# Neighbour maximum: the end of a search with other VectorE operations, a table of x with swapped blocks, and one maximum along the later ring slots

## The chip, the cores and the metric

The kernel runs on one core of one Trainium2 chip. The metric is the device time of one execution in microseconds (us); lower is better.

## What is computed

Four graph layers run over the same adjacency matrix of 8192 x 8192 (about 0.4% ones, the diagonal included) and rows x of 8192 x 128. The change lies wholly in the first layer, which takes for every row the maximum of x over the row's neighbours, adds it to x and normalises:

```python
def _L0_gnn_ref(X, adj):
    mask = adj != 0
    def body(_, mrows):
        vals = jnp.max(jnp.where(mrows[:, :, None], X[None, :, :], neg), axis=1)
        has_nbr = jnp.any(mrows, axis=1)
        return (None, jnp.where(has_nbr[:, None], vals, jnp.zeros((), X.dtype)))
...
x = _layernorm(x + _L0_gnn_ref(x, adj), axis=-1)
x = _layernorm(x + _L1_gnn_ref(x, L1_gnn_W, L1_gnn_a, adj, 8192), axis=-1)
x = _layernorm(x + _L2_gnn_ref(adj, x, L2_gnn_W, L2_gnn_a), axis=-1)
x = _layernorm(x + _L3_gnn_ref(x, adj, L3_gnn_W, L3_gnn_a), axis=-1)
```

## The kernel before

The first layer is `neighbour_max`. It walks the 64 tiles of 128 rows of the adjacency matrix, one phase for each tile. SyncE loads a tile (4 MB) in four pieces. TensorE turns it (`turn`, L470) in eight steps of eight 128x128 blocks, ScalarE makes the signs (L426) and stores them as the mask of the later layers.

The neighbours of a row are treated in two ways. Each row's columns are cut into 512 words of 16. The first neighbour in a word goes through matmuls: `firsts_of` (L489) marks it, ScalarE makes it clean (`lone`, L413), and `sum_pair` (L503) multiplies it by x in three bf16 parts into the PSUM tile `sums`. VectorE takes the maximum of `sums` and the running `top` (`pair`, L601). There are eight such pairs in a phase, called here pairs 0 to 7 (`step(0)` to `step(7)` in the code). The tile `sums` is there once, so `sum_pair` of the next pair waits on `sums_used` until VectorE has read it, and `pair` waits on `sums_ready`.

The further neighbours in a word are found by a search on VectorE, between the pairs of the phase after the tile's turning. From the counts per word it makes keys (L680 to L711), takes the eight largest words with several (L713), peels off three powers of two from each (loop over `d`, L729 to L740), and sorts the keys with MAX8 and MATCH_REPLACE8 to 24 slots (`srt`, L748 to L755). Then it works out the row numbers in `idx` (L759 to L768), which groups of slots are needed (`need`, L764), and the number found (L766). `Steps` (`steps`, `side`, `tree`) are semaphores by which one VectorE operation waits for an earlier one: `settle()` waits for all that was issued on that chain.

GpSimd gathers those rows (L352, one indirect DMA for a slot) out of `x_ext`, a copy of x in DRAM with 128 extra rows of the lowest value for empty slots, into `ring`, 24 slots of 128 values for each partition. A group of slots that no row needs is filled by a memset (L388). Two phases after the search VectorE takes the maximum over the slots: slots 0 to 11 in halves (L606, then `into`, L613), and slots 12 to 23 in the same manner in the second half of the phase, between pairs 3 and 5. `rest_ready` says that slots 12 to 23 are filled, `rest_free` that they may be filled anew.

The order on each engine is the order of the code; TensorE's is written in its `phase`, VectorE's in the `phase` below. TensorE's matmul L477, which adds up `need`, stands ahead of L489 and L503 of pair 0 of the next phase, and waits for `need_made`. In the last four phases (`quad == NC - 1`) no tile is turned any more.

The other three layers start at about 1710 us of the span and the diff doesn't touch them.

Of the kernel before, what the change touches and what calls it, by code (L numbers as in the profile page):

```python
# [8 lines left out]
I32 = mybir.dt.int32  # L9
# [3 lines left out]
ALU = mybir.AluOpType  # L13
ACT = mybir.ActivationFunctionType
AXX = mybir.AxisListType.X

P = 128
N = 8192
F = 128
T = N // P  # L20
# [3 lines left out]
NW = N // WORD  # L24
EXPONENT = 0x7F800000
TOP_BIT = 2.0 ** WORD
MORE = 8
# [50 lines left out]
def hold(eng, sem, value):  # L78


    eng.wait_ge(sem, value)
    if not isinstance(value, int):
        eng.sem_inc(SPARE[0], 1)
# [96 lines left out]
def neighbour_max(nc, x, adj, mask_t, x_ext, nm, deg, consts, constants):  # L180
# [14 lines left out]
    with ExitStack() as ctx:  # L195
# [17 lines left out]
        bit = stats[:, 0:SRT, 1].bitcast(I32)  # L213
        base = sb("base", [P, SRT], I32)
        pad = sb("pad", [P, SRT], F32)
# [112 lines left out]
        def _(pool):  # L328
# [3 lines left out]
            pool.dma_start(x_ext[P:P + N, :], x).then_inc(x_copied, 16)  # L332
            pool.wait_ge(low_ready, 1)
            pool.dma_start(x_ext[0:P, :], top[:, 0, 0:F]).then_inc(low_in, 16)
# [7 lines left out]
            pool.wait_ge(x_copied, 16)  # L342
# [224 lines left out]
        def _(dve):  # L567
# [9 lines left out]
            nc.vector.memset(top_bit[:, :], TOP_BIT).then_inc(opens_free, 1)  # L577
            steps.do(nc.vector.memset(need[:, :, :], 0.0))
# [54 lines left out]
            def between(n):  # L633

                if n == LOWEST_AT:
                    dve.wait_ge(top_used, NC - 1)
                    dve.wait_ge(lower_free, T - TC + 1)
                    dve.wait_ge(rest_free, T - TC + 1)
                if LOWEST_AT <= n < LOWEST_AT + NC - 1:
                    lowest_of(n - LOWEST_AT)  # L640
# [12 lines left out]
            def phase(t, k, extracts=True, finishes=True, quad=None, tops=True):  # L653
# [6 lines left out]
                def bits(ap):  # L660
                    return ap.bitcast(I32)
# [56 lines left out]
                if finishes:  # L718
                    hold(dve, rest_ready, old + 2)
                    tree.did(larger(h, h, h + h // 2, h // 2))  # L720
# [3 lines left out]
                if finishes:  # L724
                    tree.did(larger(h, h, h + h // 4, h // 4))
                for d in range(DEEP - 1):
                    if extracts:
                        steps.settle()
                        steps.did(nc.vector.tensor_scalar(bits(many_high[:, d, :]), bits(y), EXPONENT, None, ALU.bitwise_and))  # L729
                    if d == 0:  # L730
                        step(4)
                    if finishes and d == 1:
                        tree.did(larger(h, h, h + 1, 1))
                    if finishes and d == 2:
                        tree.did(larger(h, h, h + 2, 1))
                    if extracts:
                        steps.settle()
                        if d + 1 < DEEP - 1:
                            steps.did(nc.vector.tensor_tensor(out=y, in0=y, in1=many_high[:, d, :], op=ALU.subtract))
                        side.did(nc.vector.tensor_tensor(out=bits(keys[:, NW + d * MORE:NW + (d + 1) * MORE]), in0=bits(many_high[:, d, :]), in1=many_no[:, :], op=ALU.bitwise_or))  # L740
                if finishes:
                    tree.settle()
                    hold(dve, lower_free, old + 2)
                    into(old, None, h).then_inc(rest_free, 1)
                if extracts:
                    side.settle()
                    steps.settle()
                    steps.did(nc.vector.max(out=srt[:, 0:8], in_=keys[:, :]))  # L748
# [8 lines left out]
                if extracts:  # L757
                    steps.settle()
                    steps.did(nc.vector.tensor_scalar(bit, bits(srt[:, :]), 23, None, ALU.logical_shift_right))  # L759
                    steps.did(nc.vector.tensor_scalar(base[:, :], bits(srt[:, :]), NW - 1, 4, ALU.bitwise_and, ALU.logical_shift_left))  # L760
                    side.did(nc.vector.tensor_scalar(pad[:, :], srt[:, :], 1.0, TOP_BIT, ALU.is_ge, ALU.mult))
                    steps.settle()
                    steps.did(nc.vector.tensor_tensor(out=base[:, :], in0=base[:, :], in1=bit, op=ALU.add))
                    nc.vector.tensor_scalar(need[:, (k + 1) % 2, 0:GROUPS - SURE], srt[:, FIRST[SURE]:FIRST[-1] + 1:SIZES[SURE]], 1.0, None, ALU.is_ge).then_inc(need_made, 1)  # L764
                    side.settle()
                    side.did(nc.vector.tensor_reduce(found[:, bass.ds(s, 1)], pad[:, 0:SLOTS], axis=AXX, op=ALU.add))  # L766
                    steps.settle()
                    nc.vector.scalar_tensor_tensor(out=idx[:, (k + 1) % 2, :], in0=pad[:, :], scalar=row_no[:, 0:1], in1=base[:, :], op0=ALU.max, op1=ALU.min).then_inc(idx_ready, 1)  # L768
# [18 lines left out]
            steps.did(nc.vector.scalar_tensor_tensor(out=due[:, :], in0=due[:, :], scalar=TOP_BIT, in1=found[:, :], op0=ALU.mult, op1=ALU.not_equal))  # L787
# [1089 lines left out]
def program(nc, x, adj, W1, a1, W2, a2, W3, a3, out):  # L1877
# [4 lines left out]
    with ExitStack() as ctx:  # L1882
# [11 lines left out]
        with Phase(nc), ExitStack() as c0:  # L1894
# [6 lines left out]
            def constants(temporary):  # L1901
# [7 lines left out]
                def constants_on_pool(pool):  # L1909
# [25 lines left out]
                    s.do(nc.gpsimd.iota(row_i[:, :], pattern=[[0, 1]], base=0, channel_multiplier=1))  # L1935
# [49 lines left out]
```

## Time and profile before

| what | value |
|---|---|
| time, median of 3 runs | 4916.93 us (4913.82 to 4917.06) |
| the profiled execution's own time | 4917.19 us |
| its span | 4915.5 us |
| busy in the span | PE 4373.2, DVE 4329.7, ACT 2225.5, POOL 1240.6 us |
| TensorE clock granted, mean | 0.972 |
| first layer | 0 to about 1710 us |

Span is from the first to the last instruction; 1.7 us of the execution lie around it. The first layer is some 35% of the span. PE is TensorE, DVE VectorE, ACT ScalarE, POOL GpSimd. Busy times overlap, so they say which engines are well used, and not which of them sets the time; for that one has to look at who waits for whom inside a phase. In a timeline each row is one or more like instructions with start and duration; small VectorE instructions overlap a little (the next starts before the last has ended), so what one costs is the distance of starts, which is less than its duration.

### The profile page before, as it was taken

To read this page: it belongs to the slowest core of one execution; us is meant where nothing else is said; L and a number is where in the kernel's file an instruction comes from. 1 tells how busy PE (TensorE), PEld (TensorE's weight loads), DVE (VectorE), ACT (ScalarE), POOL (GpSimd) and SP (SyncE) were. 2 spreads that over 40 slices of the span, in tenths; PEclk is the share of its full clock that TensorE was granted. 3 is DMA by queue.
4 is the path that set the end of the run, shared out by engine and by line. 5 is a ranking of instruction groups with operands and counts; after the bars stand their busy time and mean duration, and the time that the engine had idled before them with its cause. 6 is when DMAs were issued, how large, how long until landed. Compare 5 with 4: busy or idle time off the path is not lost. (4 is left out here: it accounts for less than half of the span.)

```text
span 4915.5 us, 68122 instructions
## 1 busy us (share of the span) xinstructions
PE 4373.2 (89%) x22263; PEld 2112.3 (43%) x22263; DVE 4329.7 (88%) x7560; ACT 2225.5 (45%) x2430; POOL 1240.6 (25%) x1341
## 2 busy tenths in 40 slices
PE   4888888888888659999999997999999989999999
PEld 3444444444444233344333344444444454444444
DVE  7999999999999968888888896999999969999998
ACT  4666666666666359988889962000000010000000
POOL 6666666767667500000000000000000000000000
PEclk6999999999999979999999998999999989999999
DMA  8777777777777333333323322222222022222220
GB/s 299 246 255 249 246 255 249 254 249 256 253 248 250 103 125 129 126 114 116 120 103 129 116 89 83 75 80 81 83 81 75 23 100 86 77 77 80 103 85 7
DMA packets 181680, 709.72 MB, mean 144 GB/s; under 512 B 31152, under 2 KB 39856, under 8 KB 132208
## 3 DMA queue, kind: packets, MB, share of 16 engines
q1 hardware_dynamic: 110816, 566.01, 33.4%
q0 software_dynamic: 33744, 73.21, 4.8%
q10 hardware_dynamic: 36864, 67.13, 3.6%
q8 instruction: 157, 2.57, 0.2%
q14 instruction: 99, 0.81, 0.0%
HBM read 630.59 MB, written 79.82 MB: 145 GB/s over the span
## 5 line engine op out<-in xcount | busy, mean ns | idle before, releaser
L1743 PE MATMUL bank<-w,GX 128*128 128x512 f32 x4096 | 1767.9, 594 | 4.9 <-DVE w L1858 4.8
L1858 DVE SCALAR_TENSOR_TENSOR w<-q,E,m 128x512 f32<-128x512 f32 x2048 | 1472.6, 761 | 130.0 <-PE bank L1743 39.1
L352 POOL DMA_INDIRECT ring<-x_ext,idx x1051 | 1068.5, 1017 | 512.7 <-issue 290.7
L1743 PEld LDWEIGHTS bank<-w,GX 128*128 128x128 f32 x4096 | 778.3, 191 | 974.4 <-issue 974.3
L1193 PE MATMUL acc<-w,GX 128*128 128x512 f32 x2048 | 940.9, 606 | 66.2 <-DVE w L1451 63.0
L503 PE MATMUL sums<-lone,xs 128*128 128x512 fp8e4 x3000 | 742.2, 384 | 192.6 <-DVE top L601 174.6
L426 ACT ACTIVATE stage<-tp 128x1024 fp8e4<-128x1024 uint16 x512 | 522.7, 1022 | 507.6 <-PE tp L470 494.3
L601 DVE TENSOR_TENSOR top<-top,sums 128x1024 f32<-128x1024 f32 x484 | 587.9, 1215 | 100.3 <-PE sums L503 100.2
L1451 DVE SCALAR_TENSOR_TENSOR w<-q,E,u 128x1024 f32<-128x1024 f32 x512 | 636.7, 1282 | 1.9 <-PE acc L1193 1.8
L1193 PEld LDWEIGHTS acc<-w,GX 128*128 128x128 f32 x2048 | 372.7, 191 | 564.9 <-issue 414.3
L413 ACT ACTIVATE lone<-first_ps 128x1024 fp8e4<-128x1024 f32 x512 | 521.7, 1019 | 68.0 <-PE first_ps L489 67.3
L503 PEld LDWEIGHTS sums<-lone,xs 128*128 128x128 bf16 x3000 | 266.4, 98 | 653.8 <-issue 396.3
L1224 ACT ACTIVATE above<-q,nd 128x1024 fp8e4<-128x1024 f32 x488 | 516.6, 1141 | 0.0
L1235 ACT ACTIVATE u<-ell,ndd 128x1024 fp8e4<-128x1024 f32 x448 | 478.0, 1140 | 45.6 <-DVE w L1451 45.4
L1755 ACT ACTIVATE num<-bank 128x512 f32<-128x512 f32 x32 | 19.1, 597 | 1005.9 <-PE bank L1743 1005.9
L1708 POOL TENSOR_TENSOR lone_part<-mean_w,nohas 128x512 f32<-128x512 f32 x32 | 37.9, 1186 | 1583.2 <-DVEq L1816 1560.0
L470 PE MATMUL tp<-ident_b,adjb 128*128 128x128 bf16 x4096 | 325.6, 225 | 57.1 <-issue 23.7
L489 PE MATMUL first_ps<-stage,firsts 128*128 128x512 fp8e4 x1022 | 309.8, 385 | 0.0
L470 PEld LDWEIGHTS tp<-ident_b,adjb 128*128 128x128 bf16 x4096 | 253.6, 100 | 88.7 <-issue 32.7
L1089 POOL TENSOR_TENSOR den<-den,qcol 128x8 f32<-128x8 f32 x8 | 8.9, 1108 | 1048.6 <-ACT den L1270 1048.6
L1759 ACT ACTIVATE ex<-ex 128x512 f32<-128x512 f32 x32 | 20.2, 631 | 540.0 <-DVE ex L1817 540.0
L606 DVE TENSOR_TENSOR ring<-ring 128x128 f32<-128x128 f32 (+2 forms) x448 | 252.7, 564 | 11.3 <-DMA ring<-x_ext,idx 8.7
(248 smaller groups left out, 3299.6 us busy)
## 6 DMA issues: line engine op xcount, KB each, us to landing
adjb<-in_adj SPq DMA_DIRECT2D x256, 1024.0 KB
m<-mask_t SPq DMA_DIRECT2D x128, 1024.0 KB, 4.9
mask_t<-stage ACTq DMA_DIRECT2D x256, 256.0 KB
den_m<-mask_t SPq DMA_DIRECT2D x64, 1024.0 KB, 7.0
keep_m<-mask_t SPq DMA_DIRECT2D x64, 1024.0 KB, 5.0
ring<-x_ext,idx POOLq DMA_INDIRECT x1051
z<-row_scores SPq DMA_DIRECT2D x30, 256.0 KB, 4.7
xt_rows<-XT SPq DMA_DIRECT2D x8, 512.0 KB, 3.4
```

Source lines behind the costliest of these rows:

```text
L352: pool.indirect_dma_start(ring[:, s, :], None, x_ext, bass.IndirectOffsetOnAxis(ap=idx[:, k, s:s + 1], axis=0)).then_inc(done, 16)
L413: nc.scalar.activation(lone[:, b, :, :], first_ps[:, :, :], ACT.Relu, saturate=False).then_inc(lone_made, 1)
L426: nc.scalar.activation(stage[:, q, e * TRB:(e + 1) * TRB, k * P:(k + 1) * P], tp[e % 2][:, :, :].bitcast(U16), ACT.Sign, saturate=False).t ...
L470: last = nc.tensor.transpose(tp[e % 2][:, i, :], low_half[:, j // PW, j % PW:j % PW + P], ident_b[:, :])
L503: last = nc.tensor.matmul(out[:, a, :], xs[:, part_, 2 * n + a, :], lone[:, b, a, :], start=(part_ == 0), stop=(part_ == 2))
L601: nc.vector.tensor_tensor(out=top[:, :, :], in0=top[:, :, :], in1=sums, op=ALU.max).then_inc(sums_used, 1)
L1193: last = nc.tensor.matmul(acc[:, h, :], GX[:, j, :], w[:, n % WR1, h, :], start=(j == 0), stop=(j == T - 1))
L1224: nc.scalar.activation(above[:, n % AS, :, i, :], qb[:, c % 2, :, :], ACT.Sign, bias=nd[:, j:j + 1], scale=-1.0, saturate=False).then_inc( ...
L1235: nc.scalar.activation(u[:, n % US, :, i, :], ell[:, c % 2, :, :], ACT.Sign, bias=ndd[:, j:j + 1], saturate=False).then_inc(keeps_made, 1)
L1451: nc.vector.scalar_tensor_tensor(out=w[:, n % WR1, :, :], in0=qb[:, c % 2, :, :], scalar=E[:, j:j + 1], in1=u[:, n // GT % US, :, j % GT, ...
L1743: last = nc.tensor.matmul(acc[b][:, :], GX[:, j, :], w[:, j % WR, :], start=(j == 0), stop=(j == T - 1))
L1858: nc.vector.scalar_tensor_tensor(out=w[:, j % WR, :], in0=q, scalar=E[:, j:j + 1], in1=m[:, b, j, :], op0=ALU.max, op1=ALU.mult).then_inc( ...
```

## The change

It does four things, all in `neighbour_max`.

- **End of a search.** The seven operations that make `idx`, `need` and `found` out of `srt` become six. The three TENSOR_SCALAR on 24 elements (L759, L760, L761) and the addition (L763) become three SCALAR_TENSOR_TENSOR with a broadcast operand (`four`, `row_no`), and the last one a TENSOR_TENSOR. The sum of word address and exponent becomes an exclusive or.
- **The table.** So that the exclusive or gives the right row, the blocks of 128 rows of x lie in swapped pairs in `x_ext`, and the lowest rows at its end. The copy is made by two DMAs in place of one, GpSimd waits for both, and `row_no` counts from N.
- **Peeling.** The three TENSOR_SCALAR on 8 elements (L729) become TENSOR_TENSOR with a broadcast constant, and the three L740 one operation on 24 elements after the last of them.
- **Slots 12 to 23.** The four maxima in halves (128x768, 128x384, and two of 128x128) become one TENSOR_REDUCE over a view of the ring in which the slot runs fastest: twelve values 512 bytes apart for each of 128 outputs. It stands where the first two stood. The maximum with `nm` stays (L613), and `rest_free` is given by the reduce.

```diff
-            pool.dma_start(x_ext[P:P + N, :], x).then_inc(x_copied, 16)
+            blocks = lambda ap: ap.rearrange("(a two p) f -> a two p f", two=2, p=P)
+            for odd in range(2):
+                pool.dma_start(blocks(x_ext[0:N, :])[:, 1 - odd], blocks(x)[:, odd]).then_inc(x_copied, 16)
...
-                if finishes:
-                    hold(dve, rest_ready, old + 2)
-                    tree.did(larger(h, h, h + h // 2, h // 2))
...
                 if finishes:
-                    tree.did(larger(h, h, h + h // 4, h // 4))
+                    hold(dve, rest_ready, old + 2)
+                    nc.vector.tensor_reduce(rest_max, ring[:, h:2 * h, :].rearrange("p s f -> p f s"), axis=AXX, op=ALU.max).then_inc(rest_free, 1)
                 for d in range(DEEP - 1):
                     if extracts:
                         steps.settle()
-                        steps.did(nc.vector.tensor_scalar(bits(many_high[:, d, :]), bits(y), EXPONENT, None, ALU.bitwise_and))
+                        steps.did(nc.vector.tensor_tensor(out=bits(many_high[:, d, :]), in0=bits(y), in1=exponents[:, 0:1].to_broadcast([P, MORE]), op=ALU.bitwise_and))
                     if d == 0:
                         step(4)
-                    if finishes and d == 1:
-                        tree.did(larger(h, h, h + 1, 1))
-                    if finishes and d == 2:
-                        tree.did(larger(h, h, h + 2, 1))
...
-                        side.did(nc.vector.tensor_tensor(out=bits(keys[:, NW + d * MORE:NW + (d + 1) * MORE]), in0=bits(many_high[:, d, :]), in1=many_no[:, :], op=ALU.bitwise_or))
                 if finishes:
-                    tree.settle()
                     hold(dve, lower_free, old + 2)
-                    into(old, None, h).then_inc(rest_free, 1)
+                    hold(dve, rest_free, old + 2)
+                    tree.did(nc.vector.tensor_tensor(out=nm[:, bass.ds(old, 1), :].rearrange("p o f -> p (o f)"), in0=nm[:, bass.ds(old, 1), :].rearrange("p o f -> p (o f)"), in1=rest_max, op=ALU.max))
                 if extracts:
+                    later = keys[:, NW:NW + (DEEP - 1) * MORE].rearrange("p (d n) -> p d n", n=MORE)
+                    steps.did(nc.vector.tensor_tensor(out=bits(later), in0=bits(many_high[:, :, :]), in1=many_no[:, :].unsqueeze(1).to_broadcast([P, DEEP - 1, MORE]), op=ALU.bitwise_or))
...
-                    steps.did(nc.vector.tensor_scalar(bit, bits(srt[:, :]), 23, None, ALU.logical_shift_right))
-                    steps.did(nc.vector.tensor_scalar(base[:, :], bits(srt[:, :]), NW - 1, 4, ALU.bitwise_and, ALU.logical_shift_left))
-                    side.did(nc.vector.tensor_scalar(pad[:, :], srt[:, :], 1.0, TOP_BIT, ALU.is_ge, ALU.mult))
+                    steps.did(nc.vector.scalar_tensor_tensor(out=base[:, :], in0=bits(srt[:, :]), scalar=NW - 1, in1=four[:, 0:1].to_broadcast([P, SRT]), op0=ALU.bitwise_and, op1=ALU.logical_shift_left))
+                    side.did(nc.vector.scalar_tensor_tensor(out=pad[:, :], in0=srt[:, :], scalar=1.0, in1=row_no[:, 0:1].to_broadcast([P, SRT]), op0=ALU.is_lt, op1=ALU.mult))
+                    nc.vector.tensor_scalar(need[:, (k + 1) % 2, 0:GROUPS - SURE], srt[:, FIRST[SURE]:FIRST[-1] + 1:SIZES[SURE]], 1.0, None, ALU.is_ge).then_inc(need_made, 1)
                     steps.settle()
-                    steps.did(nc.vector.tensor_tensor(out=base[:, :], in0=base[:, :], in1=bit, op=ALU.add))
-                    nc.vector.tensor_scalar(need[:, (k + 1) % 2, 0:GROUPS - SURE], srt[:, FIRST[SURE]:FIRST[-1] + 1:SIZES[SURE]], 1.0, None, ALU.is_ge).then_inc(need_made, 1)
+                    steps.did(nc.vector.scalar_tensor_tensor(out=base[:, :], in0=bits(srt[:, :]), scalar=23, in1=base[:, :], op0=ALU.logical_shift_right, op1=ALU.bitwise_xor))
...
-                    nc.vector.scalar_tensor_tensor(out=idx[:, (k + 1) % 2, :], in0=pad[:, :], scalar=row_no[:, 0:1], in1=base[:, :], op0=ALU.max, op1=ALU.min).then_inc(idx_ready, 1)
+                    nc.vector.tensor_tensor(out=idx[:, (k + 1) % 2, :], in0=pad[:, :], in1=base[:, :], op=ALU.max).then_inc(idx_ready, 1)
```

The rows of VectorE's order say what this does to a phase. First the stretch from pair 3 to pair 5 of a phase, before the change (`ring` is the gathered slots, `X` is `nm`, the waits in brackets are semaphores of which `dve_step` is the chain `steps`):

```order
L717 TENSOR_SCALAR many_no<-many 128x8 [waits dve_step]
L606 TENSOR_TENSOR ring<-ring 128x768 [waits ring_step,rest_ready]
L723 TENSOR_TENSOR many<-many,many_no 128x8 [waits dve_step]
L606 TENSOR_TENSOR ring<-ring 128x384 [waits ring_step]
L729 TENSOR_SCALAR many_high<-many 128x8 [waits dve_step]
L601 TENSOR_TENSOR top<-top,sums 128x1024 [waits sums_ready]
L739 TENSOR_TENSOR many<-many,many_high 128x8 [waits dve_step]
L740 TENSOR_TENSOR keys<-many_high,many_no 128x8
L729 TENSOR_SCALAR many_high<-many 128x8 [waits dve_step]
L606 TENSOR_TENSOR ring<-ring 128x128 [waits ring_step]
L739 TENSOR_TENSOR many<-many,many_high 128x8 [waits dve_step]
```

The same stretch after the change, with the changed kernel's own line numbers (`merged` is the room that the reduce writes to):

```order
L723 TENSOR_SCALAR many_no<-many 128x8 [waits dve_step]
L726 TENSOR_TENSOR many<-many,many_no 128x8 [waits dve_step]
L729 TENSOR_REDUCE merged<-ring 128x128 [waits rest_ready]
L733 TENSOR_TENSOR many_high<-many,exponents 128x8 [waits dve_step]
L607 TENSOR_TENSOR top<-top,sums 128x1024 [waits sums_ready]
L739 TENSOR_TENSOR many<-many,many_high 128x8 [waits dve_step]
L733 TENSOR_TENSOR many_high<-many,exponents 128x8 [waits dve_step]
L739 TENSOR_TENSOR many<-many,many_high 128x8 [waits dve_step]
L733 TENSOR_TENSOR many_high<-many,exponents 128x8 [waits dve_step]
L743 TENSOR_TENSOR X<-X,merged 128x128 [waits rest_free,lower_free,dve_step]
L746 TENSOR_TENSOR keys<-many_high,many_no 128x24
L749 MAX srt<-keys 128x8 [waits dve_step,side_step]
```

Ahead of pair 4 the two ring maxima have become the reduce; behind it nothing of the ring stands any more between the small operations, each of which waits for the one before, and L743 now waits for the last of them too.

Then the end of a search, behind pair 7, before:

```order
L759 TENSOR_SCALAR stats<-srt 128x24 [waits dve_step]
L760 TENSOR_SCALAR base<-srt 128x24
L761 TENSOR_SCALAR pad<-srt 128x24
L763 ISA base<-stats,base 128x48 [waits dve_step]
L764 TENSOR_SCALAR need<-srt 128x3
L766 TENSOR_REDUCE nohas<-pad 128x1 [waits side_step]
L768 SCALAR_TENSOR_TENSOR idx<-pad,row_no,base 128x24 [waits dve_step]
```

and after:

```order
L760 SCALAR_TENSOR_TENSOR base<-srt,four 128x24 [waits dve_step]
L761 SCALAR_TENSOR_TENSOR pad<-srt,row_no 128x24
L762 TENSOR_SCALAR need<-srt 128x3
L764 SCALAR_TENSOR_TENSOR base<-srt,base 128x24 [waits dve_step]
L766 TENSOR_REDUCE nohas<-pad 128x1 [waits side_step]
L768 TENSOR_TENSOR idx<-pad,base 128x24 [waits dve_step]
```

The operation that makes `need` is third there in place of fifth.

## Rows read from the trace of the kernel before

**Rows 1.** Waits, 300 to 1400 us: who for whom, us in total, times, longest.

```profile
PE sums L503 <- DVE top L601: 118.6, 278, 0.8
```

**Rows 2.** Timeline of DVE, 984 to 991 us: start, duration, instruction, idle before it.

```profile
984.08 1.22 DVE L601 TENSOR_TENSOR top<-top,sums 128x1024 f32<-128x1024 f32 x1 [0.20 <-PE sums L503]
...
986.94 1.22 DVE L601 TENSOR_TENSOR top<-top,sums 128x1024 f32<-128x1024 f32 x1 [0.20 <-PE sums L503]
988.08 0.17 DVE L759 TENSOR_SCALAR stats<-srt 128x24 int32<-128x24 int32 x1
...
988.47 0.17 DVE L764 TENSOR_SCALAR need<-srt 128x3 bf16<-128x3 f32 x1
...
988.77 0.95 DVE L606 TENSOR_TENSOR ring<-ring 128x768 f32<-128x768 f32 x1
...
990.81 1.22 DVE L601 TENSOR_TENSOR top<-top,sums 128x1024 f32<-128x1024 f32 x1 [0.22 <-PE sums L503]
```

**Rows 3.** Timeline of PE in the same stretch.

```profile
988.78 0.16 PE L477 MATMUL tp<-need,ones 128*1 128x4 bf16 x1 [1.03 <-DVE need L764]
...
989.31 1.46 PE L503 MATMUL sums<-lone,xs 128*128 128x512 fp8e4 x6
```

**Rows 4.** Timeline of DVE, pairs 3 to 5 of the next phase.

```profile
999.65 1.20 DVE L601 TENSOR_TENSOR top<-top,sums 128x1024 f32<-128x1024 f32 x1
1000.77 0.16 DVE L717 TENSOR_SCALAR many_no<-many 128x8 int32<-128x8 int32 x1
1000.84 0.95 DVE L606 TENSOR_TENSOR ring<-ring 128x768 f32<-128x768 f32 x1
...
1002.30 0.30 DVE L729 TENSOR_SCALAR many_high<-many 128x8 int32<-128x8 int32 x1
1002.49 1.22 DVE L601 TENSOR_TENSOR top<-top,sums 128x1024 f32<-128x1024 f32 x1
...
1005.00 0.71 DVE L748 MAX8 srt<-keys 128x8 f32<-128x536 f32 x1
1005.63 1.20 DVE L601 TENSOR_TENSOR top<-top,sums 128x1024 f32<-128x1024 f32 x1
```

**Rows 5.** Timeline of DVE in the first search, where no pair stands between.

```profile
25.23 0.17 DVE L717 TENSOR_SCALAR many_no<-many 128x8 int32<-128x8 int32 x1
25.43 0.17 DVE L723 TENSOR_TENSOR many<-many,many_no 128x8 int32<-128x8 int32 x1
```

**Rows 6.** Groups of instructions by shape, DVE, 0 to 1640 us: count, busy us, mean ns.

```profile
L759 DVE TENSOR_SCALAR stats<-srt 128x24 int32<-128x24 int32 x63 | 29.4, 467 | 0.1
```

**Rows 7.** Timeline of DVE, the end of a search at 962 us.

```profile
961.92 1.05 DVE L759 TENSOR_SCALAR stats<-srt 128x24 int32<-128x24 int32 x1
```

**Rows 8.** Timeline of POOL: its first gather, and at 962 us.

```profile
42.40 1.08 POOL L352 DMA_INDIRECT ring<-x_ext,idx  x1 [16.42 <-PE tp L470]
...
962.03 0.90 POOL L388 MEMSET ring<- 128x256 f32 x2
```

**Rows 9.** Timeline of PE behind that end of a search.

```profile
963.43 0.16 PE L477 MATMUL tp<-need,ones 128*1 128x4 bf16 x1 [1.85 <-DVE need L764]
...
963.97 2.35 PE L503 MATMUL sums<-lone,xs 128*128 128x512 fp8e4 x6
```

**Rows 10.** Windows: busy us of each engine (x instructions), granted clock, DMA share, GB/s.

```profile
965.00:967.00 2.00, 2.00 (x13) 1.19 (x11) 0.89 (x3) 0.20 (x1) 1.33 (x2) 0.50 0.36 131
```

**Rows 11.** Groups by shape, DVE, the later layers: columns as in the sixth group.

```profile
L1007 DVE CAST kg<-rest 128x64 bf16<-128x64 f32 x3 | 0.9, 309 | 0.1
...
L1009 DVE TENSOR_TENSOR rest<-rest,kg 128x64 f32<-128x64 f32 x2 | 0.5, 272 | 0.1
L1630 DVE TENSOR_REDUCE dm<-sdh 128x1 f32<-128x64 f32 x2 | 0.5, 238 | 0.3
...
L1001 DVE TENSOR_TENSOR G<-G,v 128x64 f32<-128x64 f32 x1 | 0.2, 227 | 0.0
...
L796 DVE TENSOR_REDUCE missed<-rstd 128x1 f32<-128x64 f32 x1 | 0.2, 219 | 0.0
```

More of the change, by code:

```diff
@@ L212, in neighbour_max @@
         srt = sb("srt", [P, SRT], F32)
-        bit = stats[:, 0:SRT, 1].bitcast(I32)
         base = sb("base", [P, SRT], I32)
+        four = sb("four", [P, 1], I32)
+        exponents = sb("exponents", [P, 1], I32)
+        rest_max = merged[:, 0:F]
         pad = sb("pad", [P, SRT], F32)
@@ L331, in _ @@
             pool.wait_ge(adj_in[PIECES - 1], 16)
-            pool.dma_start(x_ext[P:P + N, :], x).then_inc(x_copied, 16)
+            blocks = lambda ap: ap.rearrange("(a two p) f -> a two p f", two=2, p=P)
+            for odd in range(2):
+                pool.dma_start(blocks(x_ext[0:N, :])[:, 1 - odd], blocks(x)[:, odd]).then_inc(x_copied, 16)
             pool.wait_ge(low_ready, 1)
-            pool.dma_start(x_ext[0:P, :], top[:, 0, 0:F]).then_inc(low_in, 16)
+            pool.dma_start(x_ext[N:N + P, :], top[:, 0, 0:F]).then_inc(low_in, 16)
             sel_steps = Steps(pool, sel_made)
@@ L341, in _ @@
                         sel_steps.do(nc.gpsimd.affine_select(out=sel[:, k, :], in_=sel[:, k, :], compare_op=ALU.not_equal, fill=1.0, base=-(at + r), pattern=[[0, 1]], channel_multiplier=1))
-            pool.wait_ge(x_copied, 16)
+            pool.wait_ge(x_copied, 32)
             pool.wait_ge(low_in, 16)
@@ L577, in _ @@
             nc.vector.memset(top_bit[:, :], TOP_BIT).then_inc(opens_free, 1)
+            steps.do(nc.vector.memset(four[:, :], 4))
+            steps.do(nc.vector.memset(exponents[:, :], EXPONENT))
             steps.do(nc.vector.memset(need[:, :, :], 0.0))
@@ L637, in between @@
                     dve.wait_ge(lower_free, T - TC + 1)
-                    dve.wait_ge(rest_free, T - TC + 1)
+                    tree.settle()
                 if LOWEST_AT <= n < LOWEST_AT + NC - 1:
@@ L786, in _ @@
             side.settle()
-            steps.did(nc.vector.scalar_tensor_tensor(out=due[:, :], in0=due[:, :], scalar=TOP_BIT, in1=found[:, :], op0=ALU.mult, op1=ALU.not_equal))
+            tree.settle()
+            steps.do(nc.vector.tensor_scalar(due[:, :], due[:, :], -1.0, float(SLOTS), ALU.mult, ALU.add))
+            steps.did(nc.vector.scalar_tensor_tensor(out=due[:, :], in0=due[:, :], scalar=row_no[:, 0:1], in1=found[:, :], op0=ALU.mult, op1=ALU.not_equal))
             lowest_of(NC - 1)
@@ L1933, in constants_on_pool @@
                         s.do(nc.gpsimd.affine_select(out=firsts_f[:, :, :], in_=firsts_f[:, :, :], compare_op=op, fill=fill, base=base, pattern=pattern, channel_multiplier=sign))
-                    s.do(nc.gpsimd.iota(row_i[:, :], pattern=[[0, 1]], base=0, channel_multiplier=1))
+                    s.do(nc.gpsimd.iota(row_i[:, :], pattern=[[0, 1]], base=N, channel_multiplier=1))
                 def constants_on_vector(dve):
```

## The prediction

> **What bounds the kernel now.** I read the waits first. Over 300 to 1400 us, some 44 phases of one tile each, the largest wait that holds work back on the two busy engines is that of TensorE's `sum_pair` on VectorE's `pair`: 118.6 us in 278 places [rows 1]. So VectorE leads where it is late, and the question is in which stretches of a phase it is. The timelines answer that. The distance from one pair to the next has a floor: pairs 6 and 7 are 2.86 us apart, and VectorE stood idle 0.20 us before the second [rows 2]. That floor is a ring of two, since `sums` is there once: 1.46 us of matmuls [rows 3], then 1.20 to 1.22 us of `pair`, and the handovers. VectorE's other work costs nothing as long as it fits beside the matmuls, that is up to 1.6 us or so between two pairs; what goes beyond is added to the phase one for one, and no later pair gives it back.
>
> Three distances matter, because the change edits only these:
>
> - Pair 3 to pair 4: 1002.49 - 999.65 = 2.84 us, no idle before it [rows 4]. This stretch stands exactly at the floor.
> - Pair 4 to pair 5: 1005.63 - 1002.49 = 3.14 us, no idle [rows 4]. Some 0.28 us above the floor.
> - Pair 7 to pair 0 of the next phase: 990.81 - 986.94 = 3.87 us, with 0.22 us idle on VectorE [rows 2]. Here a chain through TensorE is the last: `need` (start 988.47), then L477 at 988.78, after 1.03 us of idle on TensorE, L489, and the 1.46 us of L503 from 989.31 [rows 3].
>
> A whole phase without a disturbance is 24.4 us (from these distances and the others of that phase). GpSimd's gathers are not changed in number.
>
> **The reduce: the price that no row shows.** It reads 12 x 128 = 1536 values per partition. At full rate: 128x768 takes 0.95 us [rows 4] and 128x1024 1.22 us [rows 2], 1.05 ns for an element, so 0.95 + 768 x 0.00105 = 1.76 us. But the values are 512 bytes apart, and the rows say that distance costs. A TENSOR_REDUCE over 64 values 12 bytes apart takes 238 ns and one over adjacent values 219 [rows 11], 0.30 ns more per element: 1.76 + 0.46 = 2.2 us. A TENSOR_TENSOR in which one operand steps by 16 bytes takes 272 against 227 ns [rows 11], 0.70 ns per element: 1.76 + 1.08 = 2.84 us. The worst row is a CAST that writes at steps of 16 bytes, 309 ns [rows 11]; less some 150 fixed that is 2.5 ns per element, so 3.9 us. Bounds 1.76 and 3.9. I take 2.84: the row of 16 bytes is the nearer, since from 12 to 16 bytes the price more than doubles and 512 is on that side; the write row is of another port.
>
> The Trainium skill bears on this: "Vector Engine (DVE) Microarchitecture Reference", section 5.2, says that a port keeps its full rate only while the stream comes in runs of two adjacent words, and gives 1.73 ns per column where one source hops at every element (1.05 in order). By that the reduce would be an estimated 2.8 us, and the sum nearly that below. The same paragraph has a one-source stream alternating between two regions at the full rate, which would make it 1.76 us and the change about neutral. The rows of 12 and 16 bytes agree with the first.
>
> **Pair 3 to 4.** After pair 3 passes on (1.12 us, 999.65 to 1000.77 [rows 4]) come L717 and the exclusive or, which now has nothing in front of it: such a dependent step costs 0.20 us (25.23 to 25.43 [rows 5]). Then 0.08 to the start of the reduce, its 2.84 less the usual overlap of 0.09, and 0.12 for the `and`. Sum 1.12 + 0.20 + 0.08 + 2.75 + 0.12 = 4.27 us against 2.84: **+1.43**. With the bounds: +0.35 (1.76), +0.79 (2.2), +2.5 (3.9).
>
> **Pair 4 to 5.** Removed: two ring maxima of 128x128 and three small operations. But they lay in the gaps of a dependent chain, and what remains runs at 0.20 a step: four steps before L743 may start (it now waits for the last of them too) 0.80, L743 0.21, the joined operation on 24 elements 0.22, MAX8 0.63 (1005.00 to 1005.63 [rows 4]). With 1.13 for the pair: 2.99 against 3.14, **-0.15**.
>
> **Pair 7 to 0.** Seven operations from 988.08 to 988.77 cost 0.69 us [rows 2]. The six new ones: a SCALAR_TENSOR_TENSOR passes on after some 0.15, a wait for the second of them and for the third comes in, and I get about 0.73. So the short list is no shorter in time. But `need` starts 0.30 behind pair 7 in place of 0.39, and the chain through TensorE is what ends last: **-0.08** in three phases of four, and +0.04 where `merge` makes VectorE the last; -0.05 on the mean.
>
> **The blocked TENSOR_SCALARs.** L759 lasts 0.17 us when quiet [rows 2] and 0.467 on the mean [rows 6]. The difference, 0.30 us per search, is of one kind: at 961.92 it lasted 1.05 us [rows 7], until a memset of GpSimd that began at 962.03 and took 0.90 [rows 8] was over. The new operations are of forms that never show this here, except `need`, which stays a TENSOR_SCALAR, 0.30 behind pair 7 where before it stood behind the blocked ones. And the memset's place in a phase shifts with the phase. Bounds 0 and -0.30; I take half, **-0.15**.
>
> The page "SBUF — State Buffer", section "Who interferes with whom", of the Trainium skill gives the reason: one pair of ports is shared by VectorE's fast modes and GpSimd as an exclusive lock. By this rule the stall stays wherever a TENSOR_SCALAR meets a memset, which speaks for the smaller gain.
>
> **At no cost.** The two copy DMAs in place of one: GpSimd's first gather starts at 42.40 us after 16.42 us of waiting for TensorE [rows 8], which hides a further issue and some microseconds of a slower copy; without that cover it would cost what the copy is late, once. The earlier `rest_free`, two memsets, and two small operations at the layer's end: below 1 us in all. The last tiles' maxima, in phases without a search: within 2 us.
>
> **Sum.** Per phase 1.43 - 0.15 - 0.05 - 0.15 = +1.08 us. It holds in the 61 phases that have pairs, a search and a finish: +66 us. The profiled execution took 4917.19 us (span 4915.5 and 1.7 around it), which is the median of the runs within 0.3. Forecast: 4917 + 66 = **4983 us**.
>
> **The rivals.**
>
> - *Mild stride, chance 0.20.* The reduce takes 2.2 us as the row of 12 bytes has it. +0.79 - 0.35 = +0.44 a phase, +27: 4944 us. For it: it is the same operation. Against: the row of 16 bytes.
> - *The clock falls too, 0.12.* TensorE's idle ahead of pair 5's matmuls grows from about 0.4 to 1.85 us. At 963.43 it had stood idle 1.85 us; the next six matmuls took 2.35 in place of 1.46 us [rows 9, 3], and the granted clock was 0.50, the lower of its two levels, 1.2 GHz [rows 10]. Such an event costs some 1.4 us. If every third phase has one more: +28 on top, 5011 us. Against: TensorE already idles over a microsecond once in every phase [rows 3], and in most of them the clock stays up.
> - *The reduce is neutral, 0.11.* 1.76 us and half of the stalls: +0.35 - 0.35 = 0: 4917 us.
> - *The other side, 0.09.* The reduce runs at the full rate and the stall vanishes wholly. +0.35 - 0.15 - 0.05 - 0.30 = -0.15 a phase, -9, and with the stalls go the falls of the clock behind them (some ten in the timeline), -14: 4894 us. It is decided by the reduce's duration: with all stalls gone the phase gets shorter only when it stays under 1.91 us, or 2.14 with the clock's part (14 us over 61 phases) counted; above that nothing in this diff can pay for it.
> - *A port slower than any read row, 0.05.* 3.9 us: +2.5 - 0.35 = +2.15, +131: 5048 us.
> - The forecast itself, 0.43.
>
> **How the numbers follow.** 4983 is the likeliest. The range 4912 to 5022 holds the forecast with its own spread (4968 to 5000, from the stalls' 0 to -0.30 and a few clock events), the mild case, most of the clock case and half of the neutral one: 0.43 + 0.20 + 0.10 + 0.06, near 0.8. Within 0.2% (10 us) is about what a measurement of this kernel can tell from no change. Faster by more: the other side and a little of the neutral, 0.11. Within: 0.10. Slower: 0.79.
>
> **What the profile after would show.** The TENSOR_REDUCE's duration in the group of lines: 2.8 us (right), 2.2 or 1.8 (a rival). Pair 3 to 4: 4.3 us, no idle on VectorE before pair 4, and TensorE's wait on L607 larger by 1.4 us per phase. Pair 4 to 5: 2.99. A quiet pair 7 to 0: 3.79, with `need` seldom at 0.8 us. VectorE's busy time in a phase about unchanged, since it changes 2.1 us of ring maxima for a reduce of 2.8 and loses small operations. The later layers as before. What would make the forecast wrong is first the reduce's rate; then the memsets, should they fall on `need` in most phases or in none; and last a late copy of x, which would show as a wait of the first maxima on the gathers.

## The result, and the profile after

The changed kernel takes 4967.82 us (median of 4 runs, 4962.26 to 4969.10) against 4915.38 us before (4 runs, 4913.47 to 4917.06): 52 us more, ratio 1.0098 with a 95% interval of 1.0087 to 1.0110. Its profiled execution took 4967.90 us, span 4966.2 us. The forecast was 4983 us, slower, with a range of 4912 to 5022.

All of it lies in the first layer: the last pair of the layer starts at 1703.93 us before and 1756.31 after, 52.4 us later; what follows it is 1.7 us shorter, which is within the spread of the runs.

The groups of VectorE instructions of the changed kernel, by shape, 0 to 1690 us (count, busy us, mean ns, idle before):

```profile
L729 DVE TENSOR_REDUCE merged<-ring 128x128 f32<-128x1536 f32 x62 | 172.0, 2774 | 0.0
...
L723 DVE TENSOR_SCALAR many_no<-many 128x8 int32<-128x8 int32 x64 | 20.2, 316 | 0.1
...
L762 DVE TENSOR_SCALAR need<-srt 128x3 bf16<-128x3 f32 x63 | 12.9, 204 | 0.0
```

The reduce takes 2.77 us. `many_no`, a TENSOR_SCALAR that the diff does not touch, went from the 0.16 us of [rows 4] to 0.316 on the mean. The blocked operations at the end of a search ([rows 6], 467 ns) are gone but for 204 in place of some 170 ns on `need`.

The timeline of VectorE from pair 3 to pair 5, which answers to [rows 4]:

```profile
1004.70 1.20 DVE L607 TENSOR_TENSOR top<-top,sums 128x1024 f32<-128x1024 f32 x1
1005.82 0.41 DVE L723 TENSOR_SCALAR many_no<-many 128x8 int32<-128x8 int32 x1
1006.27 0.17 DVE L726 TENSOR_TENSOR many<-many,many_no 128x8 int32<-128x8 int32 x1
1006.35 2.77 DVE L729 TENSOR_REDUCE merged<-ring 128x128 f32<-128x1536 f32 x1
1009.04 0.20 DVE L733 TENSOR_TENSOR many_high<-many,exponents 128x8 int32<-128x8 int32 x1
1009.16 1.21 DVE L607 TENSOR_TENSOR top<-top,sums 128x1024 f32<-128x1024 f32 x1
...
1011.12 0.29 DVE L743 TENSOR_TENSOR X<-X,merged 128x128 f32<-128x128 f32 x1
1011.33 0.18 DVE L746 TENSOR_TENSOR keys<-many_high,many_no 128x24 int32<-128x24 int32 x1
1011.61 0.72 DVE L749 MAX8 srt<-keys 128x8 f32<-128x536 f32 x1
1012.25 1.20 DVE L607 TENSOR_TENSOR top<-top,sums 128x1024 f32<-128x1024 f32 x1
```

Pair 3 to 4 is 1009.16 - 1004.70 = 4.46 us in place of 2.84, with no idle on VectorE: between these two pairs the reduce sets the pace. Pair 4 to 5 is 3.09 in place of 3.14. And the end of the search, which answers to [rows 2]:

```profile
1017.95 1.22 DVE L607 TENSOR_TENSOR top<-top,sums 128x1024 f32<-128x1024 f32 x1 [0.19 <-PE sums L507]
1019.09 0.18 DVE L760 SCALAR_TENSOR_TENSOR base<-srt,four 128x24 int32<-128x24 int32 x1
1019.18 0.18 DVE L761 SCALAR_TENSOR_TENSOR pad<-srt,row_no 128x24 f32<-128x24 f32 x1
1019.27 0.17 DVE L762 TENSOR_SCALAR need<-srt 128x3 bf16<-128x3 f32 x1
...
1019.65 0.95 DVE L612 TENSOR_TENSOR ring<-ring 128x768 f32<-128x768 f32 x1
...
1021.62 1.22 DVE L607 TENSOR_TENSOR top<-top,sums 128x1024 f32<-128x1024 f32 x1
```

The six new operations cost 0.56 us (1019.09 to 1019.65) against 0.69. `need` starts 0.18 behind pair 7, not 0.30 as forecast: a SCALAR_TENSOR_TENSOR with a broadcast operand passes on after 0.09 us. Pair 7 to 0 is 3.67 us in place of 3.87.

The waits, 300 to 1400 us (who for whom, total us, times, longest), answer to [rows 1]:

```profile
PE sums L507 <- DVE top L607: 152.0, 259, 1.9
PE sums L507 <- ACT lone L417: 23.0, 14, 1.6
```

The first row is 33 us more than before, where the forecast had 1.4 us a phase, some 60. The rest of it stands in the second row. TensorE's idle ahead of pair 5's matmuls grew in every phase, from 0.33 us to 1.84 on the mean. Where `many_no` is quick, ScalarE's `lone` for that pair is ready no sooner than VectorE's pair (at 957.85 us and at 957.81, for matmuls that start at 957.95), and the profile puts the wait to ScalarE.

In nine phases TensorE's clock falls behind the reduce. Its timeline behind a reduce, and the window that follows (busy us per engine, granted clock 0.50, the lower level of 1.2 GHz):

```profile
983.73 2.65 PE L507 MATMUL sums<-lone,xs 128*128 128x512 fp8e4 x6 [1.95 <-DVE top L607]
```

```profile
984.00:986.00 2.00, 2.00 (x6) 0.73 (x5) 1.37 (x5) 0.00 (x0) 1.39 (x3) 0.50 0.97 395
```

The matmuls take 2.65 in place of 1.46 us after an idle of 1.95. Pairs 4 and 5 of such phases are 3.7 to 4.1 us apart.

For all kernels of this study, the mean distances between pairs, in us, worked out from the starts of L601 (or the line that answers to it) in VectorE's timeline, one trace of each kernel, over the 52 phases of quads 2 to 14 (a quad is four phases):

| kernel | 0 to 1 | 1 to 2 | 3 to 4 | 4 to 5 | 7 to 0 | phase |
|---|---|---|---|---|---|---|
| before | 3.27 | 3.01 | 2.84 | 3.15 | 4.34 | 25.28 |
| after | 3.22 | 3.06 | 4.36 | 3.20 | 3.80 | 26.30 |
| ring maxima back | 3.21 | 3.04 | 2.84 | 3.45 | 3.95 | 25.15 |
| reduce alone | 3.22 | 3.00 | 4.16 | 2.88 | 3.99 | 25.94 |
| adjacent values | 3.21 | 3.05 | 3.26 | 3.06 | 3.82 | 25.05 |
| end alone | 3.21 | 3.04 | 2.84 | 3.16 | 4.01 | 24.92 |
| peeling alone | 3.22 | 3.01 | 2.84 | 3.44 | 4.34 | 25.51 |
| after, other forms | 3.21 | 3.08 | 4.15 | 3.05 | 3.76 | 25.90 |
| end, other forms | 3.22 | 3.06 | 2.84 | 3.15 | 3.76 | 24.67 |
| and a later maximum | 3.21 | 3.06 | 2.84 | 2.92 | 3.77 | 24.45 |

The distances left out (2 to 3, 5 to 6, 6 to 7) differ by 0.03 at most. After is 1.02 us a phase longer, 53 us over these 52 phases. The other nine of the 61 phases with pairs, a search and a finish add nothing on balance: the first four and the last five pay 5.9 and 7.3 us between pairs 3 and 4, and get back 5.7 and 6.9 between pair 7 and pair 0, where before they had some of the longest stalls.

### The profile page after: what moved, and what is told of

The parts are those of the page before. It is cut to its first block and busy times, and to the rows that moved or that the text cites. A ratio compares the mean times of both kernels' runs of the same rounds, so it can differ in the third digit from the quotient of the medians.

```text
span 4966.2 us, 67679 instructions
## 1 busy us (share of the span) xinstructions
PE 4369.8 (88%) x22263; PEld 2110.9 (43%) x22263; DVE 4382.5 (88%) x7179; ACT 2219.8 (45%) x2430; POOL 1213.9 (24%) x1342
## 5 line engine op out<-in xcount | busy, mean ns | idle before, releaser
L356 POOL DMA_INDIRECT ring<-x_ext,idx x1051 | 1042.4, 992 | 592.8 <-issue 308.3
L1328 DVE SCALAR_TENSOR_TENSOR above<-above,den_m 128x1024 int32<-128x1024 int32 x128 | 156.7, 1224 | 112.3 <-ACT above L1226 88.4
```

The costliest lines, as they stand in the source:

```text
L356: pool.indirect_dma_start(ring[:, s, :], None, x_ext, bass.IndirectOffsetOnAxis(ap=idx[:, k, s:s + 1], axis=0)).then_inc(done, 16)
```

## The experiments

**The price of a step.** Nine reduces over the same 1536 values, at the end of the first layer of the kernel before; their results are thrown away.

```diff
+            flat = ring[:, HALF:2 * HALF, :].rearrange("p s f -> p (s f)")
+            tree.do(nc.vector.tensor_reduce(rest_max, flat.rearrange("p (a s) -> p a s", s=12), axis=AXX, op=ALU.max))
+            for step in (2, 3, 4, 8, 24, 32, 128):
+                tree.do(nc.vector.tensor_reduce(merged[:, 0:step], flat.rearrange("p (n a) -> p a n", a=step), axis=AXX, op=ALU.max))
+            tree.do(nc.vector.tensor_reduce(merged[:, 0:64], ring[:, HALF:2 * HALF, :].rearrange("p s (a two) -> p a s two", two=2), axis=mybir.AxisListType.XY, op=ALU.max))
```

> The kernel before with nine reduces more at the end of the first layer, each over the same 1536 values of ring slots 12 to 23 and each waiting for the one before: one over adjacent values with 128 outputs, seven whose successive values lie 2, 3, 4, 8, 24, 32 and 128 words apart (so many outputs), and one with runs of two adjacent words and then 512 bytes. Their result is thrown away. Theory A (the distance between successive values sets the price): adjacent and 2 words about 1.76 us, 3 words about 2.2, from 4 words on 2.7 to 2.9 with 128 words at 2.77 as in the changed kernel, 24 words perhaps more; runs of two 1.76. Theory B (the price comes from 128 short sums of twelve and not from the distance): the adjacent one with 128 outputs takes 2.77 too, and those with few outputs 1.76. The time of the whole is 4917 plus about 22 us for the nine.

Measured: 4941.42 us in one run, each reduce once. The groups by shape; L800 is the one over adjacent values, in L802 the number of outputs is the step in words, L803 reads runs of two:

```profile
L802 DVE TENSOR_REDUCE merged<-ring 128x24 f32<-128x1536 f32 x1 | 4.0, 3980 | 0.0
L802 DVE TENSOR_REDUCE merged<-ring 128x8 f32<-128x1536 f32 x1 | 2.9, 2895 | 0.0
L802 DVE TENSOR_REDUCE merged<-ring 128x4 f32<-128x1536 f32 x1 | 2.8, 2841 | 0.0
L802 DVE TENSOR_REDUCE merged<-ring 128x128 f32<-128x1536 f32 x1 | 2.7, 2723 | 0.0
L802 DVE TENSOR_REDUCE merged<-ring 128x32 f32<-128x1536 f32 x1 | 2.7, 2716 | 0.0
L802 DVE TENSOR_REDUCE merged<-ring 128x3 f32<-128x1536 f32 x1 | 2.2, 2169 | 0.0
L800 DVE TENSOR_REDUCE merged<-ring 128x128 f32<-128x1536 f32 x1 | 1.8, 1753 | 0.0
L802 DVE TENSOR_REDUCE merged<-ring 128x2 f32<-128x1536 f32 x1 | 1.8, 1753 | 0.0
L803 DVE TENSOR_REDUCE merged<-ring 128x64 f32<-128x1536 f32 x1 | 1.8, 1753 | 0.0
```

It is the distance, and not the number of short sums: 128 outputs cost 1.75 us with adjacent values and 2.72 with values 128 words apart. One and two words cost nothing, three 0.27 ns a value more, four and eight 0.7, 24 words 1.45, and 32 and 128 words 0.63. Runs of two adjacent words are free over a hop of 512 bytes, as the Trainium skill has it ("Vector Engine (DVE) Microarchitecture Reference", section 5.2, whose granule is two words). Where that section wants adjacent words for the full rate, this run differs: a step of two words has none, and took 1.75 us too. The section's 1.73 ns per column for a hopping source stands beside 1.67 here ((2723 - 152) / 1536, with the fixed 152 ns of [rows 11], 219 less 64 at 1.04).

**The ring maxima back.** The changed kernel with slots 12 to 23 in halves as before.

```diff
-                    nc.vector.tensor_reduce(rest_max, ring[:, h:2 * h, :].rearrange("p s f -> p f s"), axis=AXX, op=ALU.max).then_inc(rest_free, 1)
+                    tree.did(larger(h, h, h + h // 2, h // 2))
...
+                    tree.did(larger(h, h, h + h // 4, h // 4))
...
+                        tree.did(larger(h, h, h + 1, 1))
...
+                        tree.did(larger(h, h, h + 2, 1))
...
+                    into(old, None, h).then_inc(rest_free, 1)
```

> The changed kernel with the maxima of slots 12 to 23 in halves again, in their old places; all else of the change stays. Theory A (all of the loss is the reduce, and the new end of a search gains): pair 3 to 4 back at 2.84, pair 4 to 5 at about 3.2, pair 7 to 0 as in the changed kernel at 3.67, so some 0.4 us a phase under the kernel before: 4890 us (4880 to 4905), faster. Rival B (the loss comes from the small operations' chain and the new tail, the reduce only replaces equal work): it stays at 4945 to 4970.

Measured: 4902.62 us, ratio to before 0.9973 (0.9963 to 0.9983). Theory A holds in sign and place, pair 3 to 4 is back at 2.84. It gains less than the 4890 us of the forecast, though inside its range, since pair 4 to 5 is 3.45 and not 3.2, and pair 7 to 0 is 3.95 on the mean: `need` is still blocked often, 333 ns on the mean.

**The reduce alone.** The kernel before, with L729 of the changed kernel in place of the four maxima.

> The kernel before with the reduce alone; peeling, end of a search and table as before. Theory A: pair 3 to 4 at 4.2 us, pair 4 to 5 at 3.0, blocked operations at the end of a search as often as in the kernel before or more, so +1.2 us a phase: about 4985 us (4970 to 5005), slower than the changed kernel, whose new tail pays part of it back. Rival B: 4930 or less, since the reduce alone would be little.

Measured: 4946.13 us, ratio 1.0057 (1.0038 to 1.0076). It is slower, but by half of what theory A gave, and outside its range; rival B's 4930 us or less is as far off. Its VectorE timeline, pair 3, the reduce, pairs 4 and 5:

```profile
992.90 1.20 DVE L602 TENSOR_TENSOR top<-top,sums 128x1024 f32<-128x1024 f32 x1
...
994.29 2.76 DVE L724 TENSOR_REDUCE merged<-ring 128x128 f32<-128x1536 f32 x1
...
997.05 1.21 DVE L602 TENSOR_TENSOR top<-top,sums 128x1024 f32<-128x1024 f32 x1
...
999.90 1.22 DVE L602 TENSOR_TENSOR top<-top,sums 128x1024 f32<-128x1024 f32 x1
```

The price between pairs 3 and 4 is 4.15 - 2.84 = 1.31 as thought, but pair 4 to 5 comes down to the floor, 2.85. And the stall at the end of a search is nearly gone, though these operations are those of the kernel before, in its group by shape:

```profile
L754 DVE TENSOR_SCALAR stats<-srt 128x24 int32<-128x24 int32 x64 | 13.0, 203 | 0.1
```

203 ns against 467 in [rows 6], and pair 7 to 0 is 0.35 us shorter. GpSimd starts its gathers at the start of a phase and ends with the memsets, and those now lie ahead of the end of the search. Two things could do that. The phase is longer, by a reduce of 1.3 us more in its middle. And the ring is free sooner: the reduce gives `rest_free` ahead of pair 4, where before the last maximum (L613) gave it behind pair 4, and GpSimd waited for that. GpSimd's waits for the maxima that free the ring, 300 to 1400 us, before, with the reduce alone, with the ring maxima back and with adjacent values (next run):

```profile
POOL ring L352 <- DVE X L613: 25.0, 56, 1.3
POOL ring L353 <- DVE X L614: 3.3, 11, 0.3
POOL ring L356 <- DVE X L619: 21.6, 54, 0.8
POOL ring L356 <- DVE X L619: 3.4, 11, 0.3
```

The last two kernels tell the two apart. They have the same new end of a search and phases of the same length (25.15 and 25.05 us, of which 21.20 and 21.23 from pair 0 to pair 7), shorter than the 25.28 of before. They differ in when the ring is freed. With the maxima back `need` lasted over 0.25 us in 17 of the 52 phases, with the reduce in 5. So the sooner release does most of it without a longer phase, at least for the new end. How much the longer phase adds with the old end was not tried.

**Adjacent values.** The changed kernel with the reduce over twelve adjacent values: it takes the maximum of other values than the reference.

```diff
-ring[:, h:2 * h, :].rearrange("p s f -> p f s")
+ring[:, h:2 * h, :].rearrange("p s f -> p (s f)").rearrange("p (a s) -> p a s", s=h)
```

> The changed kernel with the reduce over twelve adjacent values in place of twelve values 512 bytes apart; it so takes the maximum of other values than the reference has. Theory A: the reduce takes 1.76 us, pair 3 to 4 falls from 4.16 to 4.46 us to 3.15 to 3.45, 61 times 1.01 us less: about 4906 us (4895 to 4915), faster than the kernel before by a little. Theory B (128 short sums are what is slow): 2.77 us as before and 4968 us.

Measured: 4895.72 us, ratio 0.9953 (0.9937 to 0.9969). Only the order of reading differs from the changed kernel, and it is 72 us shorter: theory A. That is more than 61 times 1.0, as the clock falls behind the reduce vanish too, and `many_no` is blocked less often (29 of 64 times against 39).

**The end of a search alone**, with its table; **the peeling alone**.

```diff
+            for odd in range(2):
+                pool.dma_start(blocks(x_ext[0:N, :])[:, 1 - odd], blocks(x)[:, odd]).then_inc(x_copied, 16)
...
-                    steps.did(nc.vector.tensor_scalar(bit, bits(srt[:, :]), 23, None, ALU.logical_shift_right))
...
+                    steps.did(nc.vector.scalar_tensor_tensor(out=base[:, :], in0=bits(srt[:, :]), scalar=NW - 1, in1=four[:, 0:1].to_broadcast([P, SRT]), op0=ALU.bitwise_and, op1=ALU.logical_shift_left))
```

> The kernel before with the new end of a search and the table that belongs to it; peeling and ring maxima as before. Theory A (this part is the gain: need is earlier and only one TENSOR_SCALAR is left that a memset can block): pair 7 to 0 quiet at 3.67 us in place of 3.87, on the mean 3.95 or less in place of 4.34, all other distances unchanged: 0.4 us a phase, 4891 us (4882 to 4902). Rival (the shortened list gains nothing, and the memsets only moved in the runs so far): 4910 to 4917.

Measured: 4892.47 us, ratio 0.9945 (0.9929 to 0.9962). Theory A: pair 7 to 0 is quiet at 3.67, the mean 4.01, and the other distances stayed within 0.06.

```diff
-                        steps.did(nc.vector.tensor_scalar(bits(many_high[:, d, :]), bits(y), EXPONENT, None, ALU.bitwise_and))
+                        steps.did(nc.vector.tensor_tensor(out=bits(many_high[:, d, :]), in0=bits(y), in1=exponents[:, 0:1].to_broadcast([P, MORE]), op=ALU.bitwise_and))
...
+                    steps.did(nc.vector.tensor_tensor(out=bits(later), in0=bits(many_high[:, :, :]), in1=many_no[:, :].unsqueeze(1).to_broadcast([P, DEEP - 1, MORE]), op=ALU.bitwise_or))
```

> The kernel before with the new peeling alone (and with a constant, and the three joined into one operation behind the ring maxima); ring maxima and end of a search as before. Theory A: pair 4 to 5 at 3.44 us in place of 3.15 as in the kernel with the ring maxima back, all else unchanged: +0.29 a phase, 4933 us (4925 to 4940), slower. Rival (three small operations less are a gain): 4905 or less.

Measured: 4927.62 us, ratio 1.0023 (1.0013 to 1.0033). Fewer operations, and slower, as theory A had it: pair 4 to 5 is 3.44. The L740 of before filled gaps in which each step waited for the last; joined into one, the operation stands in the chain, after the last `and` and the maximum with `nm`, and ahead of MAX8.

**Other forms for the blocked operations.** The changed kernel, and the kernel with the new end alone, each with `many_no` as a TENSOR_TENSOR and `need` as a SCALAR_TENSOR_TENSOR.

```diff
-nc.vector.tensor_scalar(many_no[:, :], bits(y), NW - 1, None, ALU.bitwise_and)
+nc.vector.tensor_tensor(out=many_no[:, :], in0=bits(y), in1=word_bits[:, 0:1].to_broadcast([P, MORE]), op=ALU.bitwise_and)
...
-nc.vector.tensor_scalar(need[:, (k + 1) % 2, 0:GROUPS - SURE], srt[:, FIRST[SURE]:FIRST[-1] + 1:SIZES[SURE]], 1.0, None, ALU.is_ge)
+nc.vector.scalar_tensor_tensor(out=need[:, (k + 1) % 2, 0:GROUPS - SURE], in0=srt[:, FIRST[SURE]:FIRST[-1] + 1:SIZES[SURE]], scalar=1.0, in1=ones[:, 0:1].to_broadcast([P, GROUPS - SURE]), op0=ALU.is_ge, op1=ALU.mult)
```

> The changed kernel with the two remaining small TENSOR_SCALARs of the later half of a phase in other forms: the and that makes many_no as a TENSOR_TENSOR with a broadcast constant, need as a SCALAR_TENSOR_TENSOR. Theory (these two are the ones that GpSimd's gathers and memsets block): many_no is 0.17 us in every phase where it was 0.41 in 38 of 58, pair 3 to 4 is 4.16 everywhere, need is never above 0.2, pair 7 to 0 3.67 in quiet and all other phases but the last of a quad; 0.35 us a phase less with fewer falls of the clock: 4947 us (4940 to 4957). Rival (0.41 us is another thing, such as a late key): 4965 and many_no at 0.41 still.

Measured: 4943.62 us, ratio to before 1.0050 (1.0033 to 1.0067), 24 us under the changed kernel. The groups by shape:

```profile
L763 DVE SCALAR_TENSOR_TENSOR need<-srt,ones 128x3 bf16<-128x3 f32 x64 | 10.0, 156 | 0.0
...
L724 DVE TENSOR_TENSOR many_no<-many,fixed 128x8 int32<-128x8 int32 x64 | 9.8, 153 | 0.1
```

Never blocked: 153 against 316 ns. What had blocked `many_no` is in GpSimd's timeline of the changed kernel:

```profile
1005.29 0.95 POOL L356 DMA_INDIRECT ring<-x_ext,idx  x1 [0.30 <-issue]
...
1014.96 1.16 POOL L392 MEMSET ring<- 128x256 f32 x3
```

The gather ends at 1006.24, and the `many_no` of 1005.82 (0.41 us) with it at 1006.23. The row of the memset says where the blocking of the old end of a search went: it is over at 1016.12, three microseconds before the end of this search begins.

> The kernel before with the new end of a search and its table, many_no as a TENSOR_TENSOR and need as a SCALAR_TENSOR_TENSOR; ring maxima and peeling as before. If the blocked operations are what is left to gain, it is the best of all: pair 3 to 4 at 2.84, pair 4 to 5 at 3.15, pair 7 to 0 at 3.67 (4.04 where a quad ends), so 24.66 us a phase in place of 25.28: 4878 us (4870 to 4890), faster than both kernels. Rival: the same as with the new end alone, 4891.

Measured: 4873.75 us, ratio 0.9909 (0.9892 to 0.9925), faster than both kernels. With the new end alone, `need` took 407 ns on the mean in the group by shape,

```profile
L764 DVE TENSOR_SCALAR need<-srt 128x3 bf16<-128x3 f32 x64 | 26.0, 407 | 0.0
```

since there the ring is freed as late as before, and the memsets still fall on the end of the search and block the one TENSOR_SCALAR that is left. In the other form it is 156. That bears out the rule by which the forecast kept half of the stall (the Trainium skill, "SBUF — State Buffer", "Who interferes with whom"): a TENSOR_SCALAR that meets a memset waits. What it did not tell is where the memsets would be.

**A later maximum.** The same kernel, with the last step over slots 12 to 23 written to a scratch row, which frees the ring, and its maximum with `nm` one pair later.

```diff
-                        tree.did(larger(h, h, h + 2, 1))
+                        nc.vector.tensor_tensor(out=rest_max, in0=ring[:, h, :], in1=ring[:, h + 2, :], op=ALU.max).then_inc(rest_free, 1)
...
-                    into(old, None, h).then_inc(rest_free, 1)
...
+                    if finishes and r == 1:
+                        hold(dve, lower_free, old + 2)
+                        hold(dve, rest_free, old + 2)
+                        tree.did(nc.vector.tensor_tensor(out=nm[:, bass.ds(old, 1), :].rearrange("p o f -> p (o f)"), in0=nm[:, bass.ds(old, 1), :].rearrange("p o f -> p (o f)"), in1=rest_max, op=ALU.max))
```

> The kernel before with the new end of a search, many_no and need in unblocked forms, and one change more: the last maximum over slots 12 to 23 goes to a scratch row and frees the ring, and its maximum with nm stands one pair later, between MATCH_REPLACE8 and MAX8 in the stretch from pair 5 to 6, where VectorE is idle 0.20 us anyway. Theory (a pair's distance costs only what it has above the floor of 2.85 us): pair 4 to 5 falls from 3.15 to 2.94, pair 5 to 6 stays at 2.84 to 2.87, so 0.2 us a phase less than without it: 4862 us (4857 to 4868). Rival (VectorE's work costs the same wherever it stands): 4874.

Measured: 4861.37 us, ratio 0.9888 (0.9872 to 0.9905). VectorE's timeline, pairs 4, 5 and 6:

```profile
996.62 1.22 DVE L607 TENSOR_TENSOR top<-top,sums 128x1024 f32<-128x1024 f32 x1
...
999.54 1.20 DVE L607 TENSOR_TENSOR top<-top,sums 128x1024 f32<-128x1024 f32 x1
...
1001.35 0.28 DVE L760 TENSOR_TENSOR X<-X,merged 128x128 f32<-128x128 f32 x1
...
1002.38 1.22 DVE L607 TENSOR_TENSOR top<-top,sums 128x1024 f32<-128x1024 f32 x1
```

Pair 4 to 5 is 2.92; pair 5 to 6 took the maximum in and stayed at 2.84, its idle used up. The same instruction costs 0.2 us in one place and nothing one pair later.

## Why the prediction was right, and where it was off

- **The floor of 2.85 us and VectorE's lead.** Right. Of the ten kernels none has pairs 6 and 7 nearer than 2.85, and pair 3 to 4 stands at 2.84 wherever the ring maxima are in it.
- **The reduce, 2.84 us.** It took 2.77. The row of the 16-byte step gave the right price for 16 bytes, 2.84 when measured by itself. That 512 bytes cost nearly the same was in no row, and luck had a part in it: the price does not rise or stay level in between, 24 words cost 3.98. The rivals of 1.76 and 2.2 us are the prices of steps of one or two, and of three words.
- **Pair 3 to 4, +1.43.** Quiet it was 4.16, +1.32, as the reduce and the small operations around it pass on some 0.1 us quicker than the terms had it. On the mean it was +1.53: the TENSOR_SCALAR of `many_no` was blocked in two phases of three by a gather, 0.25 to 0.3 us, which is not in the forecast. Before, 0.41 us at that place would have been hidden (with the end alone it occurs 28 times in 64, and the distance stays 2.84).
- **Pair 4 to 5, -0.15.** Quiet 3.05 to 3.09, -0.08; on the mean +0.05, with the falls of the clock.
- **Pair 7 to 0, -0.05, and the stall, -0.15.** These are the mis-sized terms: together -0.54. Quiet it gained 0.20 and not 0.08 (0.13 where a quad ends), since the SCALAR_TENSOR_TENSORs pass on after 0.09 us and not 0.15. And the stall went almost wholly: 0.35 us a phase, more than its bound of 0.30. The forecast named the sooner `rest_free` and put it, with other things, below 1 us in the whole run. But it lets GpSimd start its later gathers sooner, which moves the memsets ahead of the end of the search. Between the ring maxima back and the adjacent values, with phases of one length, pair 7 to 0 fell by it from 3.95 to 3.82, where 3.76 is what is left with nothing blocked.
- **The clock rival.** Ten times in the 61 phases of the changed kernel the six matmuls took over 1.8 us, nine of them behind idles of 1.93 to 1.95 us after the reduce, all where `many_no` was blocked; before there were 14, most of them behind stalled ends. So no third of the phases, and in the balance nothing. Each of the nine cost about 0.8 us between pairs 4 and 5 (3.88 against 3.07), and not 1.4. With `many_no` in the other form the idle there is 1.64 us and none was left; with the reduce alone it is 1.64 too, and there was none. That the shorter idle is the cause was not tried by itself.
- **The sum.** +1.08 forecast, +1.02 measured a phase. That these are so near is luck: the gain between pair 7 and pair 0 (0.34 more than forecast) hid the blocked `many_no` and the clock (0.3). Of the 14 us between 66 and 52, ten are the nine phases outside the 52, where the two cancelled wholly.
- **The parts do not add up.** Alone, against the runs of before on the same chip, they are +30 (reduce), +11 (peeling) and -24 us (end), +17 together; the change is +52. Some 24 of the 35 us between are what the other forms give back: the blocked `many_no` and the clock falls after it. That takes both parts. The reduce uses up the slack behind `many_no`, but with the reduce alone it is blocked 2 times in 64, and before 5 times; with the new end it is blocked 28 times, and in the changed kernel 39. It is blocked, with few exceptions, where it starts 0.52 us behind the start of a gather and not where it starts 1.12 behind, and which of the two it is depends on the end of the search; by what step was not tried. The rest is mostly that the reduce and the new end each claim the same stall (7 to 0: -0.35 and -0.33 alone, -0.54 together).
- **At no cost: the copy of x.** As forecast: the first gather waited 14.8 us for TensorE, and the first quad starts at 102.07 us against 101.61. The table without the new end was not tried.

## What to carry to other kernels

Count an edit by the stretch between two hand-overs in which it stands, not by the busy time it saves: two engines that share one buffer have a floor, work under it is free, and work above it is paid in full. Before replacing a tree of contiguous maxima by one reduce over a transposed view, price the step between successive values: here 2.77 us against 1.75. When an edit frees a buffer sooner, look at what the engine that waits for it will then run into, or out of. A short operation in a form that can be blocked costs nothing on the mean until the slack behind it is gone; if GpSimd gathers or fills beside it, a form with a broadcast operand was worth 24 us in one kernel and 19 in the other.

## What was not expected of the hardware

- The price of a step does not grow evenly: 1536 values take 1.75 us at 1 or 2 words, 2.17 at 3, 2.84 at 4, 2.90 at 8, 3.98 at 24, and 2.72 at 32 and at 128.
- A TENSOR_SCALAR on 8 elements lasted until the end of a gather of GpSimd that had begun 0.52 us before it (0.41 us; 39 of 39 times in the changed kernel, 5 of 8 in a gather's course before), while the TENSOR_TENSOR and SCALAR_TENSOR_TENSOR forms at the same places lasted 0.153 and 0.156 on the mean.
- SCALAR_TENSOR_TENSOR with a broadcast operand on 24 elements takes 0.18 us and passes on after 0.09, where the form with a per-partition scalar (L768 of before) takes 0.23.
